# Four projection, rotation and absorption steps spread over other head slots of a pipelined attention

## The reference

```
q = (x @ wq).reshape(b, s, 16, 192)          # per head 128 plain and 64 rotated features
kva = x @ wkv_a                              # 64 latent features and 64 rotary ones
ckv = ckv * rsqrt(mean(ckv * ckv) + EPS) * kv_norm_scale
k_nope, v = (ckv @ wkv_b) split by head
q_pe, k_pe = rope(q_pe), rope(k_pe)          # k_pe is shared by the heads
scores = (q_nope . k_nope + q_pe . k_pe) * 192 ** -0.5, causal
out = softmax(scores) @ v, heads side by side, @ wo
```

## Time and profile before

| | us |
|---|---|
| median of 3 runs | 943.53 |
| profiled execution, its own time | 944.91 |
| its span | 942.9 |
| PE / DVE / ACT / POOL busy | 856.5 / 717.7 / 531.3 / 434.7 |
| second attention, first scores | 442.8 |
| one of its batches of 16 slots | 43.0 |
| last head of its last batch turned | about 779 |

### The profile page before, as it was taken

How to read it: one execution, slowest core, us unless ns; L and a number is a source line. 1 busy time by engine, 2 the same in 40 slices (tenths; PEclk the granted TensorE clock), 3 DMA queues, 4 the chain that set the end, 5 groups by cost and what they waited for, 6 DMA issues and landing times.

```text
span 942.9 us, 19230 instructions
## 1 busy us (share of the span) xinstructions
PE 856.5 (91%) x6286; PEld 649.1 (69%) x6286; DVE 717.7 (76%) x2366; ACT 531.3 (56%) x1392; POOL 434.7 (46%) x683
## 2 busy tenths in 40 slices
PE   6678898889999999987999999999999997999996
PEld 5556666667765666655888787887888775666663
DVE  6567988889778887663968787787868686888872
ACT  5356544454354555545676676757586761555555
POOL 0348898887766665446202121221202012556655
PEclk9779999999999999989999999999999999999999
DMA  6333333332223557102112020202021022234331
GB/s 211 60 50 49 53 56 55 56 55 38 35 37 58 103 118 133 43 14 46 24 24 46 1 46 1 45 2 46 2 45 37 11 35 35 36 71 59 59 48 35
DMA packets 49938, 46.55 MB, mean 49 GB/s; under 512 B 5280, under 2 KB 47280, under 8 KB 49840
## 3 DMA queue, kind: packets, MB, share of 16 engines
q1 hardware_dynamic: 49840, 45.33, 26.2%
HBM read 11.40 MB, written 2.10 MB: 14 GB/s over the span
## 4 chain that ended last, share of the span: by engine, by line
PE 33%; DVE 15%; issue 3%; ACT 1%; POOL 1%; DMA 0%; POOLq 0%; SPq 0%; DVEq 0%; ACTq 0%
PE bank L301 8%; PE bank L1979 6%; PE bank L1987 4%; PE bank L1913 4%; DVE weights L1476 3%; PE bank L1928 3%; DVE weights L1466 3%; PE bank L1743 2%; PE bank L1756 2%; DVE q_lo L1456 1%; PE bank L1739 1%; DVE rope L1454 1%; PE bank L1782 1%; DVE xn L338 1%; DVE arena L1313 1%
## 5 line engine op out<-in xcount | busy, mean ns | idle before, releaser
L1313 DVE TENSOR_REDUCE arena<-bank 128x2 f32<-128x512 f32 (+1 forms) x192 | 130.9, 685 | 42.4 <-PE bank L1743 41.4
L924 ACT ACTIVATE weights<-bank 128x512 f32<-128x512 f32 x144 | 85.8, 596 | 109.1 <-PE bank L1756 108.3
L1006 ACT ACTIVATE weights<-weights,neg_max 128x128 f32<-128x128 f32 (+1 forms) x256 | 113.9, 449 | 39.2 <-DVE neg_max L1466 38.7
L727 POOL TENSOR_SCALAR_AFFINE_SELECT weights<-weights 128x256 f32<-128x256 f32 x144 | 68.6, 478 | 101.4 <-ACT weights L924 101.4
L1979 PE MATMUL bank<-kbT,arena 128*128 128x128 f32 (+1 forms) x512 | 105.1, 328 | 1.0 <-DVE y L447 0.9
L667 POOL TENSOR_SCALAR weights<-weights 128x512 f32<-128x512 f32 x64 | 97.6, 1537 | 12.5 <-ACT weights L832 12.5
L1743 PE MATMUL bank<-kf_stack,q_stack 96*128 96x256 f32 (+1 forms) x256 | 99.7, 432 | 0.0
L1013 ACT ACTIVATE weights<-bank 128x384 f32<-128x384 f32 x128 | 62.7, 490 | 61.0 <-PE bank L1987 60.5
L1466 DVE CUSTOM_DVE_ANT_0 weights<-bank,arena 128x128 f32<-128x128 f32 (+1 forms) x256 | 80.2, 350 | 14.6 <-PE bank L1979 12.6
L301 PE MATMUL bank<-x_hi,wb_hi 128*128 128x256 f32 x256 | 83.8, 327 | 2.8 <-DVE q_lo L1456 2.8
L1476 DVE TENSOR_SCALAR weights<-weights,inv_sum 128x128 f32<-128x128 f32 (+1 forms) x256 | 81.3, 360 | 4.6
(11 more groups left out here) (236 smaller groups left out, 2514.2 us busy)
## 6 DMA issues: line engine op xcount, KB each, us to landing
q_stack<-q_hi SPq DMA_DIRECT2D x96, 128.0 KB, 4.5
arena<-arena SPq DMA_DIRECT2D x64, 128.0 KB, 2.5
q_stack<-q_lo SPq DMA_DIRECT2D x48, 128.0 KB, 5.3
ka_stack<-k_hi SPq DMA_DIRECT2D x32, 76.5 KB, 2.8
x_all<-x SPq DMA_DIRECT2D x8, 256.0 KB, 5.1
st_wo<-b_wo SPq DMA_DIRECT2D x8, 256.0 KB, 4.2
arena<-b_wqn SPq DMA_DIRECT2D x8, 256.0 KB, 3.3
out<-x_all SPq DMA_DIRECT2D x8, 256.0 KB, 2.1
```

Source lines behind the costliest of these rows:

```text
L924: a.activation(s["pT"][(STEPS * b + k) % N_PT], p2[k % 2][:, :], ACT.Exp).then_inc(s["exp"], 1)
L1006: last = a.activation(p, p, ACT.Exp, scale=-1.0, bias=neg_max[:, h % 4, t:t + 1], accum_out=sums[:, h % 4, t:t + 1])
L1313: v.tensor_reduce(into, p1[k % 2][:, :].rearrange("p (s g k) -> p s g k", s=n, g=NC), AX.X, ALU.max, negate=True).then_inc(s["maxed"], 1)
```

## The change

Group i of the rotary queries was projected by PE in slots 4, 5, 6, 7; now in slots 3, 5, 6, 7, so the first follows `kva` at once. DVE multiplied in the same slots; it now does so in its slots 4, 6, 7, 8 (`TURN_SLOTS`), and POOL one slot after each. DVE takes `kva` out in slot 4 and not 3, and makes the keys in slot 10 and not 5; POOL does its parts in slots 5 and 11 and not 4 and 6. Transposition and copy of the keys are in slot 12 and not 8. The absorbed groups are in slots 9, 11, 13, 15 and not 9, 10, 11, 12. PE's waits are changed to fit the new order of the banks. On ACT `act_ctx` now stands ahead of `copy_probs`, and on DVE `low_oT` ahead of `step_b`. No operation is added or left out.

```diff
--- before.py
+++ after.py
@@ -54,8 +54,9 @@
 
 
 
-ROPE_SLOTS = {4: 0, 5: 1, 6: 2, 7: 3}
-ABS_SLOTS = {9: 0, 10: 1, 11: 2, 12: 3}
+ROPE_SLOTS = {3: 0, 5: 1, 6: 2, 7: 3}
+TURN_SLOTS = {4: 0, 6: 1, 7: 2, 8: 3}
+ABS_SLOTS = {9: 0, 11: 1, 13: 2, 15: 3}
 QUADS = H // 4
 PROJECTED = {0: ("k", 1), 1: ("q", 0), 2: ("q", 1)}
 BUSY = {(-2, 11): 2, (-2, 15): 5, (-1, 7): 3, (-1, 10): 2, (-1, 12): 2, (-1, 14): 1}
@@ -742,17 +743,17 @@
                 return step
 
             def step_b(b, par, h):
-                if h == 4:
+                if h == 5:
                     wait_apart(pool, *at(sm, "kva", b, 3))
                     g.tensor_scalar(rms[:, :], sq_sum[:, :], 1.0 / LORA, EPS_RMS, ALU.mult, ALU.add)\
                         .then_inc(sm["rms"], 1)
                     pool.wait_ge(*at(sm, "rms", b, 1))
                     g.tensor_tensor(rms[:, :], rms[:, :], expo[:, :], ALU.pow).then_inc(sm["rms"], 1)
-                if h == 6:
+                if h == 11:
                     pool.wait_ge(*at(sm, "k_tok", b, 2))
                     g.tensor_copy(kv_tok[par][:, :, W_ABS:], kv_tok[par][:, :, 0:LORA]).then_inc(sm["k_odd"], 1)
-                if h - 1 in ROPE_SLOTS:
-                    i = ROPE_SLOTS[h - 1]
+                if h - 1 in TURN_SLOTS:
+                    i = TURN_SLOTS[h - 1]
                     pool.wait_ge(*at(sm, "qr_dve", b, i + 1))
                     if i == 0:
                         pool.wait_ge(*at(sm, "q_got", b, 0))
@@ -995,7 +996,7 @@
                         last = a.activation(qT[par][rows, 4 * i + j:4 * i + 4:2, :],
                                             halves((ps_b, ps_a)[i % 2])[rows, :, :], ACT.Copy)
                     last.then_inc(sm["qa_out"], 1)
-                if h == 8:
+                if h == 12:
                     act.wait_ge(*at(sm, "kT_ps", b, 1))
                     a.activation(kbT[par][:, :, :], halves(ps_a), ACT.Copy, scale=-SCALE_B).then_inc(sm["kT"], 1)
 
@@ -1030,11 +1031,11 @@
                         exps_b(b + 1, 0)
                     if h != 2 and b + 1 < B:
                         step_b(b + 1, 1 - b % 2, h)
-                    copy_probs(b, h)
                     if h % 4 == 0 and h > 0:
                         act_ctx(b, h // 4 - 1)
                     elif h == 0 and b > 0:
                         act_ctx(b - 1, QUADS - 1)
+                    copy_probs(b, h)
                     if b == B - 1:
                         for n in steps_beside_b(h):
                             step_g(*n)
@@ -1425,7 +1426,7 @@
             def step_b(b, par, h):
                 if h == 2:
                     dve_x_lo(sm, b)
-                elif h == 3:
+                elif h == 4:
                     dve.wait_ge(*at(sm, "kva_ps", b, 1))
                     link(sm, "kva", b, 1, v.tensor_copy(kva_tok[:, :, :], halves(ps_b)[:, :, 0:W_ABS]))
                     for t in range(NT):
@@ -1433,7 +1434,7 @@
                         v.tensor_tensor_reduce(out=k_rot[:, 0, t, :], in0=lat, in1=lat, scale=1.0, scalar=0.0,
                                                op0=ALU.mult, op1=ALU.add,
                                                accum_out=sq_sum[:, t:t + 1]).then_inc(sm["kva"], 1)
-                elif h == 5:
+                elif h == 10:
                     dve.wait_ge(*at(sm, "kva", b, 3))
                     wait_since(dve, sm, "o_ps", b - 2, QUADS)
                     link(sm, "k_tok", b, 1, rotary((k_rot[:, 0], k_rot[:, 1]), kva_tok[:, :, LORA:W_ABS],
@@ -1444,8 +1445,8 @@
                         last = v.scalar_tensor_tensor(kv_tok[par][:, t, 0:LORA], kva_tok[:, t, 0:LORA],
                                                       rms[:, t:t + 1], norm_bc[:, :], op0=ALU.mult, op1=ALU.mult)
                     last.then_inc(sm["k_tok"], 1)
-                if h in ROPE_SLOTS:
-                    i = ROPE_SLOTS[h]
+                if h in TURN_SLOTS:
+                    i = TURN_SLOTS[h]
                     bank = halves((ps_a, ps_b)[i % 2])
                     dve.wait_ge(*at(sm, "qr_ps", b, i + 1))
                     dve.wait_ge(*at(sm, "qr_out", b, i))
@@ -1504,12 +1505,12 @@
                     elif b + 1 < B:
                         maxima_b(b + 1, 0)
                     normalize_probs(b, h)
-                    if b + 1 < B:
-                        step_b(b + 1, 1 - b % 2, h)
                     if h == 1 and b > 0:
                         low_oT(b - 1, QUADS - 1)
                     elif h % 4 == 1 and h > 1:
                         low_oT(b, h // 4 - 1)
+                    if b + 1 < B:
+                        step_b(b + 1, 1 - b % 2, h)
                     if h == 3 and b > 0:
                         residual_b(b - 1)
                     if h == 12 and b + 2 < B:
@@ -1950,8 +1951,8 @@
                     for x in range(2):
                         last = mm3(halves((ps_a, ps_b)[i % 2])[:, x, :], cols(WB, W_PE + (2 * i + x) * P, P), cols(X, 0, T))
                     last.then_inc(sm["qr_ps"], 1)
-                if h == 8:
-                    pe.wait_ge(*at(sm, "qr_dve", b, 3))
+                if h == 12:
+                    pe.wait_ge(*at(sm, "qa_out", b, 2))
                     pe.wait_ge(*at(sm, "k_odd", b, 1))
                     for j in range(2):
                         for t in range(NT):
@@ -1961,9 +1962,9 @@
                 if h in ABS_SLOTS:
                     i = ABS_SLOTS[h]
                     if i < 2:
-                        pe.wait_ge(*at(sm, ("qr_dve", "kT")[i], b, (4, 1)[i]))
+                        pe.wait_ge(*at(sm, "qr_dve", b, 4 - i))
                     else:
-                        pe.wait_ge(*at(sm, "qa_out", b, i - 1))
+                        pe.wait_ge(*at(sm, ("qa_out", "kT")[i - 2], b, 1))
                     for j in range(2):
                         last = mm3(halves((ps_b, ps_a)[i % 2])[:, j, :], cols(WB, W_ABS + (2 * i + j) * P, P), cols(X, 0, T))
                     last.then_inc(sm["qa_ps"], 1)
```

## The result

The changed kernel takes 946.01 us (median of 20 runs, 943.21 to 947.08), the kernel before 942.62 in 20 runs; the ratio is 1.0029, interval 1.0019 to 1.0038 (the ratio is not the quotient of the medians, which is 1.0036). It is slower by 0.3%, within the 0.5% that the forecast called no change; the forecast was 944.8 us. The profiled execution has a span of 944.5 us and an own time of 946.54, 1.6 above that of before. One execution of a later run, e4_batch0_old, took 1595.81 us where its eleven others took 940.51 to 943.54; it is counted in that run's median and not in its ratio.

What follows compares the result with a forecast made beforehand. The prediction took PE to bound the second attention stage. Its terms, 944.9 + 0.7 (steady batches) + 1.5 (batch 0) - 0.9 (last batch) = 946.2, less 1.4 for the median, gave 944.8 us, range 934 to 952.

Steps and rivals of the forecast that it cites:

- Absorbed groups at 9, 11, 13, 15: Steady batches: waits in slots 14 and 15 go, -1.02 us; slot 0 loses 0.89 to ACT's copy behind an evacuation.
- Key transposition to slot 12: Steady batches, slot 12: the transposition waits for an ACT evacuation, 0.46 us lost; the copy allows the attention product equally late.
- Slots 4 and 8: Steady batches: attention products there lose the PE work in front of them, costing 0.05 us each, 0.10 together.
- Rotary groups: Steady batches, slots 4 to 10: spreading rotations removes slot 7's lateness, -0.33 us; no bank waits in slots 7 or 9.
- Local orders: `act_ctx` and `low_oT` moved forward: about 0.8 us earlier, worth -0.9 us in the last batch (0 to -1.5).
- Batch 0: Prepared beside the layer before: transposition, its evacuation wait and last evacuation 0.5 us each, +1.5 (-1 to +3.5).
- A: Rival, faster: evacuations do not hold up slots 0 and 12, only gains remain, 934 us; chance 0.17.
- B: Rival, slower: evacuations before copy, exponentials and normalisation make heads late, +7 us, 952; chance 0.16.
- C: Rival, slower by the clock: the new 0.9 us pause in slot 0 lowers PE's clock, +21 us, 966; chance 0.05.

Runs made afterwards that it cites:

- e4_batch0_old: The changed kernel, but batch 0 keeps the slots of the kernel before: 941.58 us, ratio 0.9990 to the kernel before.
- e1: The changed kernel, but in slot 15 ACT copies the head before the evacuation of absorbed group 3: 938.59 us, ratio 0.9964.
- e10: The changed kernel with absorbed groups in slots 9, 10, 13, 14 instead of 9, 11, 13, 15: 937.30 us, ratio 0.9939.
- e6: The changed kernel with key transposition and its copy in slot 10, DVE's keys in slot 9, batch 0 unaltered: 947.79 us, ratio 1.0047.
- e7: The changed kernel, but in slot 11 ACT copies the head before the evacuation of absorbed group 1: 950.15 us, ratio 1.0073.
- e3: The changed kernel with both local orders of the kernel before, so only the slots are changed: 945.13 us, ratio 1.0020.
- e2: The kernel before with only the two local orders of the changed one, all slots as before: 940.58 us, ratio 0.9986.
- e11: The kernel of e5, but batch 0 has the new slots for keys, key transposition and absorbed groups: 936.01 us, ratio 0.9923.
- e12: The kernel of e5, but batch 0 has the new slots for rotary groups, rotations and kva: 934.64 us, ratio 0.9910.
- e5: The changed kernel with batch 0's old slots, key transposition in slot 10, and ACT's copy before evacuation in slots 11 and 15: 931.64 us, ratio 0.9895.

## Why the prediction was right

The mechanism held: the waits that the change removes and the two that it creates on ACT were found, and they cancel. That the total came out so near is in part luck, since two errors of the sum cancel as well (below).

*Absorbed groups at 9, 11, 13, 15.* The waits of slots 14 and 15 are gone, as forecast (-0.42 and, with its 1.42 of new work, -0.59). The wait in slot 0 was forecast at 0.89 and is 3.46 - 2.57 = 0.89; e1 shows by taking it away that it is the copy's place behind the evacuation, and that nothing is late behind it. e10 agrees, where no evacuation precedes an attention product.

*Key transposition to slot 12.* Forecast 0.46, measured 3.53 - 3.02 = 0.51 (slot 8 of the kernel before, 3.02, has the same work without the wait). That the copy allows the attention product at the same moment was in the working, and e6 shows it: with the transposition gone the slot stays at 3.46. e7 shows the other side.

*Slots 4 and 8.* Forecast +0.05 each; both are at 2.58. 4.00 less a group of 1.42 is 2.58, and 3.02 less the 0.43 that the key transposition adds to slot 10 in e6 is 2.59. The term is nothing.

*Rotary groups.* Slot 7 lost its wait (2.75 to 2.42) and no rotation is waited for in 7 or 9. SP's DMAs begin 25.09 us after the batch's first scores against 24.34 in the kernel before: 0.75 later, where the working had about 6, in a term that costs nothing. Not seen was slot 6, 4.02 to 3.84: it too held about 0.2 of lateness behind `low_oT`, without a releaser in PE's timeline (DVE ends it at 589.26, PE's output projection begins at 589.31). e3 shows that the slots take this away and not the local order. These two errors, of 0.10 and 0.18, less some 0.1 in slots 3 and 12, are why a steady batch gained 0.08 where the sum had +0.10, 1.0 us in all (-0.30 against +0.7).

The working calls the stage bound by PE. PE's waits in slots 3 to 7 are small, but the chain of waits there is DVE's (see e2): the two need about the same time. The forecast took no harm, since the change spreads DVE's work too; where it is not spread, in e2, the expected 0.996 did not come.

*Local orders.* Forecast -0.9 in the last batch, measured -1.18, and e3 gives it back (+1.17). `low_oT` starts 2.19 us after the attention product of slot 0, against 3.04 before: 0.85 earlier, the forecast had 0.8. That they serve no steady batch with the new slots is shown by e3 too (42.86).

*Batch 0* is the term that was mis-sized: +1.5, measured +2.94. The first step that failed is the end of PE's wait, which the working left at 429.4: it came at 430.43, and 1.10 later counted from `kva`. What moved behind it cost 1.84 where three terms of 0.5 stood. e4 shows that the slots make the whole; how it divides between keys and absorbed groups on one side and rotary groups on the other e11 and e12 leave open.

*The whole.* The profiled executions differ by 1.6 us, and the sum had +1.3. That is nearer than its terms are: batch 0 was 1.4 too low, and the steady and the last batches together 1.3 too high (1.0 and 0.3). This part of the agreement is luck.

The medians differ by 3.4. The profiled execution of before was a long one of its kernel (944.91 against a median of 942.62). The clocks on record say more. Beside the experiments the kernel before ran 53 times: 30 times with a mean granted clock of 0.974 or more, median 942.2 us, and 18 times with 0.971 or less, median 944.8. The changed kernel had 0.974 once in 20 and 0.971 or less 13 times, median 946.5. At the lower clocks the two are 1.7 apart, as the profiled ones are (0.971 and 0.970); the rest of the 3.4 goes with the higher clock, which the changed kernel is seldom granted. What in the change takes it is not shown. The sum was made against a profile at the lower clock, and the forecast of 944.8 is 1.2 short.

*The rivals.* A falls: the two waits were paid in full. But e1, e10 and e5 show that its size was there to be had with another order on ACT. B falls: no head was late, neither in the changed kernel nor in e1, where the exponentials stand behind the evacuation. C falls: with a pause of 0.81 us in slot 0 the steady batches keep a granted clock of 1.00 (448 to 745 us). The rule of the Trainium skill, TensorE: Matmul & The Clock Gate, named with that rival does not show in the steady batches here. Outside them the clock did take a part, as said above. For rival A one thing is to be set right: that the banks alternate is read from the program, since the trace names them all `bank`.

## What to carry to other kernels

When work is spread over the slots of a pipeline, lay out for each slot what the *other* queues do next after the moved piece: here two evacuations of 1.2 us came to stand in front of the copies that an attention product waits for, and that cost what the spreading won. An edit of one line in the order of a queue then decides the sign (0.9964 against 1.0029), and the same line in slot 11 costs 0.4%. Look behind the wait that the trace names for the next one of the same length, and give the first batch, which is prepared beside other work, a plan of its own (e4: 0.9990 with it, 1.0029 without).

## What the runs showed of the hardware

The granted clock before the first head was not the same from one execution to the next. It was 0.80 to 0.92 in the mean of 404 to 446 us, and fell to 0.50 for stretches of 3.4 or 6.8 us. From `kva` to the first scores the old slots took 30.33 to 31.45 us, the new ones 32.84 to 34.29.

The same pause is not always followed by the lower clock. PE idled 2.05 or 2.06 us before absorbed group 0 in the kernel before, e2, e4 and e5; in the first three a stretch of 3.4 us at 0.50 followed, in e5 none.

In steady batches pauses of 0.3 to 1.0 us (after, e6, e7) left the granted clock at 1.00. With e5_all the profile shows PE busy for 41.47 of 41.47 us there.

An ACT copy of 64 rows takes as long as one of 128: in the changed kernel 592 ns in the mean for 64x512 (L996) and 597 for 128x512 (L431). So an evacuation in two halves costs two whole ones, 1.19 us.

A pair of DVE `tensor_scalar` of 128 and 256 columns took 1.02 to 1.03 us beside a POOL `tensor_tensor` and 0.55 without one (e2).
